# State space scan: the norm's roots placed before the copy of B, batch 1's step sizes issued one instruction at a time

## The reference

```
x = x + _L1_attn_ref(_layernorm(x), Wi_f, conv_w_f, ..., Wo_b)      # forward and backward scan, halved sum
# inside, for each direction:
dt = jax.nn.softplus(dt + dt_bias)                                   # the "step sizes", 4 heads
def step(h, inp):
    dA = jnp.exp(dt_t * A)                                           # A = -exp(A_log)
    h = h * dA[..., None, None] + (dt_t[..., None] * x_t)[..., None] * B_t[:, None, None, :]
    y_t = jnp.einsum('bhpn,bn->bhp', h, C_t)
# layernorm: (x - m) / sqrt(v + eps), on every row
```

## Time and profile before

| | us |
|---|---|
| median of 3 runs (823.7 to 825.31) | 824.1 |
| the profiled execution | 819.01 |
| its span | 817.2 |
| TensorE busy | 715.5 |
| ScalarE busy | 542.0 |
| VectorE busy | 489.4 |
| GpSimd busy | 275.2 |

### The profile page before, as it was taken

One profiled execution on the slowest core, in us unless ns is written; L12 is line 12 of the kernel. 1 busy time (PEld: TensorE's weight loads), 2 busy tenths in 40 slices (PEclk: granted clock), 3 DMA queues, 4 the chain that ended last, 5 costly groups with the idle time before them and its releaser, 6 DMA issues. The chain is left out here.

```text
span 817.2 us, 13088 instructions
## 1 busy us (share of the span) xinstructions
PE 715.5 (88%) x4076; PEld 377.9 (46%) x4076; DVE 489.4 (60%) x1424; ACT 542.0 (66%) x934; POOL 275.2 (34%) x296
## 2 busy tenths in 40 slices
PE   4799999979999997988988867798888987999996
PEld 1432222212223223555655545576575775566564
DVE  6878442204766565763466649789697875533453
ACT  5367998888998993653357666885987642434441
POOL 3090003301000342435522445343443380265552
PEclk9899999999999997999999988899998898999999
DMA  4056934521493311112121031121211231222233
GB/s 136 1 203 165 186 86 88 207 76 53 138 317 85 110 37 40 44 34 62 42 80 46 26 109 60 52 65 53 74 60 50 81 84 39 65 61 57 67 99 92
DMA packets 76409, 70.10 MB, mean 86 GB/s; under 512 B 9687, under 2 KB 60233, under 8 KB 76080
## 3 DMA queue, kind: packets, MB, share of 16 engines
q1 hardware_dynamic: 71024, 60.56, 26.6%
q0 software_dynamic: 5024, 8.54, 3.2%
q10 hardware_dynamic: 288, 0.10, 0.0%
HBM read 41.23 MB, written 29.02 MB: 86 GB/s over the span
## 5 line engine op out<-in xcount | busy, mean ns | idle before, releaser
L693 ACT ACTIVATE attn_p<-attn_ps 128x1024 f32<-128x1024 f32 x256 | 241.1, 1083 | 28.5 <-PE attn_ps L686 17.2
L709 PE MATMUL attn_ps<-attn_p,attn_v 128*32 128x512 f32 x1024 | 138.1, 611 | 5.5 <-issue 5.5
L1687 PE MATMUL ps_main<-moe_xsT,moe_w 128*128 128x320 f32 x384 | 127.9, 459 | 8.5 <-DVE moe_hid L1712 3.3
L1697 ACT ACTIVATE moe_act_h<-ps_main 128x320 f32<-128x320 f32 (+1 forms) x128 | 55.2, 434 | 102.5 <-PE ps_main L1687 72.2
L1712 DVE TENSOR_TENSOR moe_hid<-moe_act_h,ps_main 128x320 f32<-128x320 f32 (+1 forms) x128 | 61.9, 485 | 91.1 <-ACT moe_act_h L1697 57.4
L1580 POOL DMA_INDIRECT moe_slots<-rows,moe_scatter_at x64 | 63.4, 991 | 103.0 <-DVE moe_hid L1712 53.8
L1687 PEld LDWEIGHTS ps_main<-moe_xsT,moe_w 128*128 128x128 f32 x384 | 68.8, 195 | 42.5 <-issue 21.8
L686 PE MATMUL attn_ps<-attn_q_rows,attn_k_rows 64*128 64x512 bf16 x448 | 80.6, 388 | 6.4 <-issue 3.1
L1717 PE MATMUL ps_main<-moe_hid,moe_w 128*128 128x320 f32 (+1 forms) x256 | 73.3, 451 | 4.6 <-DVE moe_hid L1712 4.6
L686 PEld LDWEIGHTS attn_ps<-attn_q_rows,attn_k_rows 64*128 64x128 bf16 x448 | 19.1, 93 | 124.0 <-ACT attn_p L693 99.0
L2119 DVE SCALAR_TENSOR_TENSOR mb_act<-mb_padded,mb_taps,mb_act 128x1024 f32<-128x1024 f32 x48 | 65.9, 1382 | 9.0 <-ACT mb_act L2110 8.3
(11 more groups left out here) (268 smaller groups left out, 1304.5 us busy)
## 6 DMA issues: line engine op xcount, KB each, us to landing
mb_cums<-mb_cum_kept SPq DMA_DIRECT2D x32, 256.0 KB, 3.4
moe_slots<-zeros SPq DMA_DIRECT2D x4, 1380.0 KB, 13.4
attn_q_rows<-attn_q_parts SPq DMA_DIRECT2D x36, 128.0 KB
attn_k_rows<-attn_k_parts SPq DMA_DIRECT2D x36, 128.0 KB
moe_w<-in_w SPq DMA_DIRECT2D x3, 1536.0 KB, 11.6
moe_rows<-zeros SPq DMA_DIRECT2D x4, 1024.0 KB, 14.7
moe_back<-moe_rows SPq DMA_DIRECT2D x16, 256.0 KB, 3.8
mb_e_cum<-mb_e_cum_kept SPq DMA_DIRECT2D x56, 64.0 KB, 2.7
```

Source lines behind the costliest of these rows:

```text
L693: self.core.nc.scalar.activation(self.p[:, w % self.PB, :, :].rearrange("p a n -> p (a n)"), self.ps_s[:, w % self.SB, :, :].rearrange("p ...
L709: ins = self.core.nc.tensor.matmul(self.ps_av[32 * i:32 * i + 32, :], self.v[:, b * TPB + kt, (HGROUPS * i + m) // 2, self.window(m)], sel ...
L1687: self.core.nc.tensor.matmul(ps[:, w % 2, 0:CAP], wt[:, e, c * P:(c + 1) * P], self.xsT[:, u % 2, :], start=True, stop=True).then_inc(self ...
L1697: self.core.nc.scalar.activation(self.act_h[into, w % 2, :], self.ps_h1[rows, w % 2, 0:CAP], ACT.Silu).then_inc(self.silu_done, 1)
```

## The change

On ScalarE `exps` is cut in two, `lower` (the Relus) and `raise_exps` (copy of B, Exp). At position 6 of units 0 and 2 the two roots are now issued between them; before they stood behind both. On batch 1's step sizes: TensorE's `steps` and VectorE's part 0 move from position 1 to 0 of unit 1, ScalarE's `exp_dt` from 2 to 1, `sums` from 3 to 4 and `exp_sums` from 4 to 5. Parts 1 to 3 are replaced by 15 links `step_link(k)`, k = 0 to 14. At positions 1, 2 and 3 VectorE issues one link in each of four places: behind `front`, behind `pass_state`, behind `back`, and at the end of the round. The last place of position 3 issues links 11 to 14 together. Each link first waits for the chain. Link 0 also waits for `exp_dt`. Batch 0's step sizes, which are taken under the MoE before the scan, stay as they are.

```diff
@@ -2030,6 +2030,7 @@
         ins.then_inc(self.norm_done, 1)
 
     STEP_PARTS = 4
+    LINKS = 4
 
     def step_sizes(self, dve, ch, b, part):
 
@@ -2073,6 +2074,46 @@
 
 
 
+    def step_link(self, dve, ch, b, k):
+
+        nc, tiles, every = self.core.nc, slice(b * TPB, (b + 1) * TPB), [P, TPB, 2 * NH]
+        v, ex, sq, poly = self.v, self.ex, self.sq, self.poly
+        terms = list(range(self.LOG_TERMS - 1, 0, -1))
+        ch.wait()
+        if k == 0:
+            dve.wait_ge(self.dt_exp, b + 2)
+            ch.step(nc.vector.tensor_scalar(poly[:], ex[:], 2.0, None, ALU.add))
+        elif k == 1:
+            ch.step(nc.vector.reciprocal(poly[:], poly[:]))
+            ch.step(nc.vector.tensor_scalar(v[:], v[:], 0.0, None, ALU.max))
+        elif k == 2:
+            ch.step(nc.vector.tensor_tensor(ex[:], ex[:], poly[:], ALU.mult))
+        elif k == 3:
+            ch.step(nc.vector.tensor_tensor(sq[:], ex[:], ex[:], ALU.mult))
+        elif k == 4:
+            ch.step(nc.vector.tensor_scalar(poly[:], sq[:], 1.0 / (2 * self.LOG_TERMS + 1), None, ALU.mult))
+        elif k < 5 + len(terms):
+            ch.step(nc.vector.scalar_tensor_tensor(poly[:], poly[:], 1.0 / (2 * terms[k - 5] + 1), sq[:], ALU.add, ALU.mult))
+        elif k == 5 + len(terms):
+            ch.step(nc.vector.scalar_tensor_tensor(poly[:], poly[:], 1.0, ex[:], ALU.add, ALU.mult))
+        elif k == 6 + len(terms):
+            ch.step(nc.vector.scalar_tensor_tensor(self.dt[:, tiles, :], poly[:], 2.0, v[:], ALU.mult, ALU.add))
+        elif k == 7 + len(terms):
+            for di in range(2):
+                of = slice(di * NH, (di + 1) * NH)
+                ins = nc.vector.scalar_tensor_tensor(self.a[:, b, di, :, :], self.dt[:, tiles, of], -1.0, self.a_exp[:, of].unsqueeze(1).to_broadcast([P, TPB, NH]),
+                                                     ALU.mult, ALU.mult)
+            ins.then_inc(self.a_done, 1)
+
+    def step_links(self, dve, ch, g, place):
+
+        u, i = g // self.NC, g % self.NC
+        if u == 1 and 1 <= i <= 3:
+            self.step_link(dve, ch, 1, (i - 1) * self.LINKS + place)
+            if (i, place) == (3, self.LINKS - 1):
+                for k in range(3 * self.LINKS, 7 + self.LOG_TERMS):
+                    self.step_link(dve, ch, 1, k)
+
     def project(self, pe, u, c):
         di, b = self.UNITS[u]
         weight = self.w_xbc[:, di, c, :] if c < 4 else self.w_z[:, di, c - 4, :]
@@ -2148,6 +2189,10 @@
 
 
     def exps(self, act, g):
+        self.lower(act, g)
+        self.raise_exps(act, g)
+
+    def lower(self, act, g):
 
         nc = self.core.nc
         u, di, b, i, n, cols = self.at(g)
@@ -2158,6 +2203,10 @@
         for hh in range(NH):
             ins = nc.scalar.activation(self.e_seg[:, g % 2, hh, :], self.cums[:, g % 2, hh, :], ACT.Relu, bias=self.cum[:, di, n, hh:hh + 1], scale=-1.0)
         ins.then_inc(self.lowered, 1)
+
+    def raise_exps(self, act, g):
+
+        nc = self.core.nc
         act.wait_ge(self.b_done, g + 1)
         if g >= 2:
             act.wait_ge(self.st_done, self.passed(g - 2))
@@ -2470,9 +2519,9 @@
                     if u == 0 and i == 7:
                         norm.turn(pe, 18)
                         norm.turn(pe, 19)
-                    if u == 1 and i == 1:
+                    if u == 1 and i == 0:
                         mamba.steps(pe, 1)
-                    if u == 1 and i == 3:
+                    if u == 1 and i == 4:
                         mamba.sums(pe, 1)
                     if u == 2 and i == 7:
                         norm.turn(pe, 20)
@@ -2655,10 +2704,13 @@
                     u, i = g // NC, g % NC
                     if g + 1 < N:
                         mamba.front(dve, g + 1)
+                    mamba.step_links(dve, ch, g, 0)
                     mamba.pass_state(dve, g)
+                    mamba.step_links(dve, ch, g, 1)
                     if g == 1:
                         dve.wait_ge(moe.y_out[(HALF - 1) % moe.OUT], moe.landings(HALF - 1))
                     mamba.back(dve, g)
+                    mamba.step_links(dve, ch, g, 2)
                     if u >= 1 and i == 1:
                         mamba.variance(dve, u - 1)
                     if u == 3 and i == GROUP + 1:
@@ -2680,11 +2732,9 @@
                     if u == 0 and i == 6:
                         norm.normalise(dve, ch, 18)
                         norm.normalise(dve, ch, 19)
-                    if u == 1 and i == 1:
+                    if u == 1 and i == 0:
                         mamba.step_sizes(dve, ch, 1, 0)
-                    if u == 1 and i == 2:
-                        for part in range(1, mamba.STEP_PARTS):
-                            mamba.step_sizes(dve, ch, 1, part)
+                    mamba.step_links(dve, ch, g, 3)
                     if u == 2 and i == 4:
                         norm.stats_of(dve, ch, 20)
                         norm.stats_of(dve, ch, 21)
@@ -2784,15 +2834,13 @@
                 for g in range(N):
                     u, i = g // NC, g % NC
                     if g + 1 < N:
-                        mamba.exps(act, g + 1)
+                        mamba.lower(act, g + 1)
+                        if i == mamba.GATES_AT and u in (0, 2):
+                            norm.root(act, 18 + u)
+                            norm.root(act, 19 + u)
+                        mamba.raise_exps(act, g + 1)
                     if g == 1:
                         act.wait_ge(moe.y_out[(HALF - 2) % moe.OUT], moe.landings(HALF - 2))
-                    if u == 0 and i == mamba.GATES_AT:
-                        norm.root(act, 18)
-                        norm.root(act, 19)
-                    if u == 2 and i == mamba.GATES_AT:
-                        norm.root(act, 20)
-                        norm.root(act, 21)
                     gates = u + 1 < UNITS and i == mamba.GATES_AT
                     if g >= 1 and not gates:
                         mamba.square(act, g - 1)
@@ -2813,9 +2861,9 @@
                     if u == 0 and i == 7:
                         norm.copy(act, nc.scalar.copy, 18)
                         norm.copy(act, nc.scalar.copy, 19)
-                    if u == 1 and i == 2:
+                    if u == 1 and i == 1:
                         mamba.exp_dt(act, 1)
-                    if u == 1 and i == 4:
+                    if u == 1 and i == 5:
                         mamba.exp_sums(act, 1)
                     if u == 2 and i == 7:
                         norm.copy(act, nc.scalar.copy, 20)
```

## The result

The changed kernel took 828.87 us (median of 22 runs, 819.52 to 834.58). The kernel before, run beside it on the same chip, took 823.67 (22 runs, 818.03 to 826.94). The ratio is 1.0047, with an interval of 1.0025 to 1.0069: slower by about 3.9 us, 2.1 to 5.7. The forecast had 0.3 us and its range ended at +3.1.

A forecast was written before the change was run, and what follows sets the result against it. VectorE was taken to bound unit 1 to position 5, ScalarE position 6 of each unit. Roots -0.76 and block 15 +1.08 gave +0.3 us, so 824.1 became 824.4 us; whole range 822.1 to 827.2.

The forecast's parts named there:

- What bounds the kernel: VectorE's own work sets the pace in unit 1 to position 5; ScalarE does at position 6 of each unit.
- Part one: Roots move into ScalarE's wait for B, units 0 and 2: copy to Silus 3.52 us, not 3.90; -0.76 us in all.
- The new wait: Unit 1, position 1: VectorE waits 2.02 us for exp_dt before link 0, as exp_dt stands behind ScalarE's first tap.
- VectorE's balance: Unit 1: new wait 2.02, less 1.43 saved by spacing, plus 0.22 of lost overlap, gives +0.81 us.
- The spacing: VectorE, unit 1: twelve links standing single between other instructions save 0.12 us each, 1.43 in all.
- rival 3: VectorE's links: spacing saves nothing, each costs its chained 0.26 us; 825.8 us, slower; chance 0.08.
- The sums: Unit 1, position 4: TensorE waits about 2 us for the step sizes; block 15 comes 1.08 us later.
- rival 1: Clock falls behind the new waits; behind the sums' wait 1.7 us is paid in full: 826.1 us; chance 0.30.
- The sum: Whole kernel: -0.76 for the roots and +1.08 for unit 1 give +0.3 us.

The follow-up runs named there:

- part one alone: The kernel before with only the roots moved between the Relus and the copy of B and Exp; ratio 1.0009 to the kernel before.
- Exp first: The changed kernel with exp_dt ahead of ScalarE's take and first tap at position 1 of unit 1; ratios to the kernel before 0.9966 and 1.0035.
- filled kernel: The changed kernel with four unread matrix products in TensorE's wait before batch 1's sums; ratio 1.0041 to the kernel before, 825.11 us.
- dense: The changed kernel with exp_dt ahead of take and first tap, and links closer, the last at position 3; ratios to the kernel before 0.9972 and 0.9997.
- With filler: Unread matrix products in TensorE's Silu waits before blocks 8, 16 and 24, added to the closer-links kernel (ratio 0.9944) and to the kernel before (1.0006).

## Why the prediction was wrong

**What bounds the kernel** was read rightly up to the sums. Where VectorE's stretch became 2.5 us shorter with the same gap behind it (33.68 + 4.01 against 31.20 + 4.00), TensorE's block 15 came earlier by as much. Behind the sums TensorE ended last, as forecast.

**Part one** was right to the hundredth, 3.90 to 3.52 in unit 0 and in unit 2 (625.82 to 629.34), and the Exp's own load stood where it was put. Of -0.76, unit 0's -0.38 appears in every kernel with the moved roots. In the changed kernel unit 2's was given back: block 23 to 24 took 10.13 in both runs, against 9.96 before, since the clock was low from block 23's turn on (0.66 us for its first pair, 0.41 before, where it fell only in the output products behind it) and its copy of B came 1.33 us behind its turn, not 0.78. In part one alone and in five of the others with the moved roots it took 9.58, as summed; in the two of Exp first, 10.14.

**The new wait** was right in kind and place, and too small: 2.62 and 2.36 us in the two runs, not 2.02. Three terms were off. Part 0 took 542.09 - 541.70 = 0.39, not 0.56: its second instruction has 0.22 us here and had 0.38 before, for which no row shows a reason. `steps` waited 0.17 for its bank at 537.46. And the take and tap were not simply 1.81 later: the take waited for its piece until 543.53, and then again for the second half. VectorE's balance was +1.35 to +1.6, not +0.81.

**The spacing** was right. With the wait removed unit 1 took 31.20 in place of 32.34, 1.1 less, where the sum had 1.21. In the changed kernel link 5 goes from start to next start in 553.97 - 553.83 = 0.14:

```profile
553.40 0.18 DVE L2094 TENSOR_SCALAR mb_poly<-mb_sq 128x64 f32<-128x64 f32 x1
553.50 0.41 DVE L2286 TENSOR_TENSOR mb_h<-mb_h_dec,ps_main 128x256 f32<-128x256 f32 x1
553.83 0.21 DVE L2096 SCALAR_TENSOR_TENSOR mb_poly<-mb_poly,mb_sq 128x64 f32<-128x64 f32 x1
553.97 0.41 DVE L2319 TENSOR_TENSOR mb_y_old<-mb_e_cum,ps_main 128x256 f32<-128x256 f32 x1
```

By the rule of the Trainium skill ("VectorE: DVE Perf Modes", section "The DRAIN you can't avoid") a link would cost the same alone as chained, and rival 3 would have shown about 32.34 + 0.22 = 32.6 without the wait. The runs at 31.2, and the 0.14 above against 0.26 chained, are against it here.

**The sums, the step that failed.** I gave 0.42 to a clock that stays up behind the sums' wait and 0.30 to rival 1, left the clock out of the sum, and argued for this that the wait, 2.03 us, is shorter than the 2.92 that drew the clock down before. The trace of the kernel before had a case between: the turn of block 23 waited 2.58 us, and the output products behind it ran slow.

```profile
618.66 0.41 PE L2141 MATMUL ps_main<-ident,mb_act 128*128 128x128 f32 x2 [2.58 <-DVE mb_gm L2188]
...
621.30 1.06 PE L2251 MATMUL ps_main<-mb_act,mb_h 128*128 128x128 f32 x4
```

A wait of 2.29 us at block 16 of the same trace didn't draw it, so a shorter wait settled nothing either way. All five traces with the 2.03 us wait show it down; filled, or absent, it stays up. So rival 1 held, in its mechanism and its place. Its price was also too low. 1.7 us was the loss of the stretch in before; measured against the filled kernel's gap of 0.90 it was 2.55 - 0.90 = 1.65 in the first run, but 4.01 - 0.90 = 3.11 in the second, and 3.1 in both traces of the kernel with the Exp first. With the clock held up the gap of 0.90 is close to the forecast's own terms: 0.76 of before, and the 0.25 by which TensorE (570.9) was to end behind VectorE (570.65), so 1.01.

**The sum.** For unit 1 up to block 15: +1.08 forecast; measured 33.96 + 2.55 and 33.68 + 4.01 against 33.08 and 33.11, thus +3.4 and +4.6. Less 0.38 from unit 0 that is +3.0 to +4.2, around the +3.9 of the timed runs. The range's upper end took rival 1 with its 1.7 and left out the case in which the clock stays low for longer. Blocks 7 to 31 of the first pair of traces show only +2.35, since block 8 to 9, ahead of this stretch, happened to take 3.56 in the changed kernel and 4.96 before; that is chance, not a gain.

What stays open. The timed differences on one chip (4.65 us for the Exp first, 5.02 for the filler) are larger than the 2.5 and 3.1 in the traces; one trace per kernel doesn't show the mean over runs. The intervals of these ratios to the kernel before touch that of the changed kernel (1.0056 to 1.0129). Set against it directly, on that chip, the means lie 4.6 us (Exp first), 4.5 (filler) and 8.4 (dense) below it, with standard errors of 1.2 to 1.4. So that each cause costs time is shown; how much each costs is known to 2 or 3 us. When exactly the clock falls and how long it stays down isn't settled: at block 16 a wait of 2.64 or 2.65 us for the Silus was followed by a low clock in four traces and not in three. That the filled kernel's blocks 7 to 31 took 151.45 isn't explained in each of its parts; 5.93 of it was block 8 to 9.

## What to carry to other kernels

When work is moved earlier, ask of each helper engine not whether its result could be ready but what stands ahead of it in that engine's list: here an Exp of 0.24 us behind one take and tap held VectorE for 2.62 us, and moving it ahead of them gave that back. Spread chained instructions singly between independent ones, each saves about 0.12 us of 0.26, but check that the last of them still comes before its reader. And price a wait of TensorE with what follows it at the lower clock: in a chain where TensorE ends last, a wait of 2 us cost up to 3 us more behind it, and useless products in it gave that back.

## What the runs showed of the hardware

A wait of TensorE of 2.03 us, in a stretch where it was busy before and behind, was followed in five traces of five by a fall to 1.2 GHz, and one of 2.74 or 2.92 us in four of four: the output products behind block 14's turn took 1.06 us instead of 0.61, and the 6 us behind part one's wait had a granted clock of 0.50. The 0.31 us that the filler left didn't draw it.

The wait for the last Silu at block 8 did so in every trace that came to it at full clock without filler: eight of eight, 2.65 us, block 8 to 9 then 4.92 to 5.93 us. With filler, at full clock too, it took 3.56 and 3.55. Where the clock had fallen in block 7 instead, it cost nothing in three of four traces (3.55 or 3.56), since ScalarE sets the pace of block 7. At block 16 the same wait drew the clock in four traces of seven. This is much of what makes single traces of this kernel differ, and why a gain of 1 us has to be read from a stretch that repeats (VectorE's unit 1, 32.32 and 32.36) and not from the span.
